# Keeping a feed-forward tile in two PSUM banks, half-width scans and new call orders in a one-core adaLN / attention / feed-forward kernel

## Time and profile before

| | us |
|---|---|
| median of 3 runs (lowest, highest) | 225.58 (223.62, 227.23) |
| the profiled execution: its time, and the span of its instructions | 226.96, 225.0 |
| DVE busy | 190.0 |
| ACT busy | 173.5 |
| PE busy (its matmuls' ends are modelled) | 150.2 |
| POOL busy | 149.4 |

### The profile page before, as it was taken

How to read it: one execution, slowest core, us unless ns; L and a number is a source line. 1 busy time by engine, 2 the same in 40 slices (tenths; PEclk the granted TensorE clock), 3 DMA queues, 4 the chain that set the end, 5 groups by cost and what they waited for, 6 DMA issues and landing times.

```text
span 225.0 us, 2670 instructions
## 1 busy us (share of the span) xinstructions
PE 150.2 (67%) x692; PEld 104.0 (46%) x692; DVE 190.0 (84%) x287; ACT 173.5 (77%) x297; POOL 149.4 (66%) x172
## 2 busy tenths in 40 slices
...
GB/s 199 361 423 143 82 245 0 3 0 0 6 90 0 0 0 0 0 4 0 1 1 0 0 0 3 0 3 1 0 0 1 3 0 0 1 23 25 34 36 70
DMA packets 5439, 9.89 MB, mean 44 GB/s; under 512 B 817, under 2 KB 3505, under 8 KB 5169
## 3 DMA queue, kind: packets, MB, share of 16 engines
...
q10 hardware_dynamic: 368, 0.03, 0.1%
...
## 4 chain that ended last, share of the span: by engine, by line
POOL 15%; PE 13%; issue 10%; DVE 6%; ACT 6%; DVEq 0%; POOLq 0%; ACTq 0%
PE banks L1533 12%; POOL qr L441 2%; POOL wn L498 2%; DVE own L1303 2%; PE banks L1530 2%; POOL grs L441 1%; POOL h L467 1%; ACT junk_q L818 1%; POOL gq L490 1%; DVE Fs L1101 1%; POOL qfl L491 1%; POOL dec L411 1%; ACT w2T L630 1%; POOL qmv L439 1%; POOL stdf L486 1%
## 5 line engine op out<-in xcount | busy, mean ns | idle before, releaser
L411 POOL TENSOR_TENSOR dec<-tri,la 128x1024 f32<-128x1024 f32 x8 | 16.9, 2112 | 15.5 <-DVE la L1179 14.5
L1533 PE MATMUL banks<-inw,uT 128*128 128x8 f32 (+1 forms) x64 | 21.7, 465 | 4.5 <-DVE uT L1147 3.9
L1101 DVE TENSOR_TENSOR_SCAN Fs<-D,E 128x1028 f32<-128x1028 f32 x8 | 18.4, 2320 | 4.6 <-POOL D L375 3.8
L1109 DVE TENSOR_TENSOR_SCAN Ys<-D,Fs 128x1028 f32<-128x1028 f32 x8 | 22.2, 2806 | 0.0
L1533 PE MATMUL banks<-dec,late 128*128 128x512 f32 x32 | 20.0, 754 | 1.8 <-POOL dec L411 1.8
L1533 PE MATMUL banks<-uT,inw 128*128 128x256 f32 x80 | 20.6, 402 | 0.0
L1190 DVE SCALAR_TENSOR_TENSOR cv<-banks,cols,cv 128x255 f32<-128x255 f32 (+2 forms) x48 | 19.2, 473 | 0.1
L1120 DVE SCALAR_TENSOR_TENSOR nd<-Ys,gap,own 128x512 f32<-128x512 f32 x16 | 18.5, 1205 | 0.0
L1533 PE MATMUL banks<-outw,yzT 128*128 128x256 f32 x64 | 16.6, 416 | 2.1 <-ACT yzT L771 2.1
L1533 PE MATMUL banks<-wabs,ones 128*128 128x2 f32 x2 | 0.6, 347 | 25.3 <-ACT dec L618 25.3
L1533 PEld LDWEIGHTS banks<-uT,inw 128*128 128x128 f32 x80 | 15.6, 202 | 3.9 <-issue 2.0
(11 more groups left out here) (176 smaller groups left out, 484.6 us busy)
## 6 DMA issues: line engine op xcount, KB each, us to landing
...
```

What stands on the lines that cost most here:

```text
L411: pool.tensor_tensor(dec[:, c], tri[:].unsqueeze(1).broadcast_to([P, NH, P]), la[:, b % 2, c, :].unsqueeze(2).broadcast_to([P, NH, P]), AL ...
L1101: dve.tensor_tensor_scan(Fs[:, w], D[:, w, 0:L], E[:, b % 2].rearrange("p k c t -> p (k c t)"), 0.0, ALU.mult, ALU.add).then_inc(fs_ok, 1)
L1109: dve.tensor_tensor_scan(Ys[:, w][:, ::-1], D[:, w, 1:L + 1][:, ::-1], Fs[:, w][:, ::-1], 0.0, ALU.mult, ALU.add).then_inc(ys_ok, 1)
L1533: return pe.matmul(dst, lhsT, rhs, start=start, stop=stop)
```

## The change

Four things, all in one edit:

1. Scans in halves. `D` holds one row of decays for both sums (514 + 1), `starts` is half as long, and `forward(b, w, k)`, `backward(b, w, k)` scan 514 elements. `forward(b, w, 0)` waits for `emin_ok` alone, not for POOL's product. `tn` has memory of its own, and `forward` no longer waits for `recip`.
2. The feed-forward tile stays in PSUM. `ffn_mid(i)` is two neighbouring banks. PE writes both halves there and adds `b1` as `diag x b1b` in float32, where `diag` is the identity scaled by `1/al1` (ACT `ffn_diag`; `ral1` comes from one reciprocal more in `ffn_in_back`). ACT's silu takes `al1` as its scale and works in place, gelu too, and `ffn_center` as well; `ffn_center` now waits for `ffn_var` of its own tile. `ffn_shift` reads PSUM and writes `Y`, which takes `U`'s place in `wn`. `ffn_u` is gone.
3. Every bank of `HOME` is new.
4. All five lists are new: the loads' order, two table loads fewer (26), and PE's waits that keep banks apart, among them seven of the form `pe.wait_ge(Y_ok, n)`, which hold PE until `ffn_shift` of tile `n - 1` is done.

```diff
@@ memory and helpers
+        def ffn_mid(i):
+            home = HOME["ffn_up"][i]
+            return banks[:, home:home + 2, :].rearrange("p a n -> p (a n)")
-        starts = sb("starts", [P, CT, T], BF16)
+        starts = sb("starts", [P, T], BF16)
-        D = sb("D", [P, 2, L + 1])
+        D = sb("D", [P, 2, CT * TS + 1])
-        tn = Fs[:, 0, 0:2 * CT * T].rearrange("p (w t) -> p w t", w=2)
+        tn = sb("tn", [P, 2, CT * T])
-        U = wn[:, 0].rearrange("p (i f) -> p i f", i=2)
-        G, Y = GY[:, :, 0], GY[:, :, 1]
+        Y = wn[:, 0].rearrange("p (i f) -> p i f", i=2)
+        diag = sb("diag", [P, 2, P])
+        ral1 = sb("ral1", [P, NT])
-    "ffn_up": ((3, 6), (5, 2), (7, 3), (4, 7), (6, 4), (3, 7), (1, 4), (5, 6)),
+    "ffn_up": (0, 2, 0, 0, 2, 0, 4, 2),
@@ ACT
+            def ffn_diag(i):
+                act.wait_ge(ident_ok, 2)
+                act.wait_ge(al1_ok, 2 * (i // TT + 1))
+                if i >= 2:
+                    act.wait_ge(h_ps, i - 1)
+                act.activation(diag[:, i % 2], ident[:], ACT.Copy, scale=ral1[:, i:i + 1]).then_inc(dg_ok, 1)
             def ffn_silu(i):
-                act.wait_ge(U_ok, 2 * (i + 1))
-                act.activation(U[:, i % 2], U[:, i % 2], ACT.Silu).then_inc(S_ok, 1)
+                act.wait_ge(h_ps, i + 1)
+                act.activation(ffn_mid(i), ffn_mid(i), ACT.Silu, scale=al1[:, i:i + 1]).then_inc(S_ok, 1)
...
@@ DVE
-            def forward(b, w):
-                dve.wait_ge(ev_ok, b + 1)
+            def forward(b, w, k):
+                if k == 0:
+                    dve.wait_ge(emin_ok, b + 1)
+                else:
+                    dve.wait_ge(ev_ok, b + 1)
...
-                if b >= 1:
-                    dve.wait_ge(rn_ok, seeds(b))
-                dve.tensor_tensor_scan(Fs[:, w], D[:, w, 0:L], E[:, b % 2].rearrange("p k c t -> p (k c t)"), 0.0,
-                                       ALU.mult, ALU.add).then_inc(fs_ok, 1)
+                dve.tensor_tensor_scan(Fs[:, w, k], D[:, w, 0:CT * TS],
+                                       E[:, b % 2, k].rearrange("p c t -> p (c t)"), 0.0, ALU.mult,
+                                       ALU.add).then_inc(fs_ok, 1)
...
+                dve.reciprocal(ral1[:, TT * b:TT * b + TT], al1[:, TT * b:TT * b + TT]).then_inc(al1_ok, 1)
-            def ffn_u(i, g):
...
             def ffn_center(i):
                 dve.wait_ge(nmu_ok, i + 1)
+                dve.wait_ge(gvar_ok, i + 1)
                 dve.wait_ge(lng_in, 16)
+                dve.scalar_tensor_tensor(ffn_mid(i), ffn_mid(i), nmu[:, i:i + 1], lngb, ALU.add, ALU.mult)\
+                    .then_inc(W_ok, 1)
...
             def ffn_shift(i):
...
-                dve.scalar_tensor_tensor(Y[:, i % 2], lnbb, std[:, i:i + 1], Y[:, i % 2], ALU.mult, ALU.add)\
+                dve.scalar_tensor_tensor(Y[:, i % 2], lnbb, std[:, i:i + 1], ffn_mid(i), ALU.mult, ALU.add)\
                     .then_inc(Y_ok, 1)
@@ PE
+            def ffn_up(i):
                 pe.wait_ge(wT_ok[0], 1)
                 pe.wait_ge(q1T_ok, i // TT + 1)
+                pe.wait_ge(b1_in, 16)
+                for g in range(2):
+                    half = slice(g * 512, (g + 1) * 512)
+                    for k in range(CT):
+                        mm(ffn_mid(i)[:, half], q1T[:, k, i * P:(i + 1) * P], w1T[:, k, half], k == 0, False)
+                pe.wait_ge(dg_ok, i + 1)
+                for g in range(2):
+                    half = slice(g * 512, (g + 1) * 512)
+                    last = mm(ffn_mid(i)[:, half], diag[:, i % 2], b1b[:, half], False, True)
                 last.then_inc(h_ps, 1)
```

More of the change, by code:

```diff
@@ L581, in _ @@
             ffn_round(5)
+            ffn_dev(7)
             ffn_rms(6)
-            ffn_dev(7)
+            ffn_rms(7)
             ffn_round(6)
-            ffn_rms(7)
             ffn_round(7)
@@ L999, in _ @@
             ffn_var(4)
-            ffn_turned(2, 0)
+            ffn_diag(6)
             ffn_var(5)
```

761 lines of the change are left out of this document (376 added, 385 removed).

## The result

The changed kernel takes **213.09 us** (median of 4, 212.26 to 213.75) against 226.41 (223.62 to 227.8) in the same runs: a ratio of 0.949, 95% interval 0.940 to 0.958. The prediction was 220.7 (212 to 230): the median fell by 13.3 us where 4.9 were forecast, to where the third rival put it. The profiled execution took 213.06; its span is 211.2 against 225.0. The kernel before has two kinds of executions, near 223.7 us at a mean granted clock of 0.92 and near 227 us at 0.89: the profiled one is of the second kind, as most are, so some 3 of the 13.8 us between the two spans go with its lower clock, and the ratio compares the quicker executions alone.

What follows compares the result with a forecast made beforehand. The bound was read as DVE from 14 to 60 us, PE from 123, ACT from 165 to 187, then latency; 1.1 - 3.5 + 1.0 + 0.5 - 4.0 = -4.9 off the median 225.58 gave 220.7 us, range 212 to 230.

Steps and rivals of the forecast that it cites:

- third rival: Whole kernel: DVE is the pacemaker throughout, so its 9.5 us saved count in full; 212.7 us, chance 0.20.
- First part: 14 to 98 us, DVE full: same instructions in another order, half scans +1.9, shorter first_D -0.8; sum +1.1 us.
- The start: First scan up to 2 us sooner, but POOL's own_times_v(0) falls among the scans; together costed at nothing.
- half scans: DVE's scans: splitting adds 0.16 us each, +1.9 for batches 0 to 2 and +0.6 for batch 3.
- 98 to 123 and 123 to 147 us: DVE's wait filled and ffn_u(0) gone, -3.5; then PE full to 165, float32 matmuls against earlier la, net +1.0.
- The hole: Near 102 us: DVE waits 3.57 us for batch 2's features; work moved ahead of that wait was to fill it.
- 147 to 187: ACT full: diags and scale columns +2.7, cheaper make_D; PE's added matmuls covered, if thinly; +0.5 taken.
- The end: From gelu(4) on: two table loads fewer, shift unheld, round(7) starts at 27.6 instead of 31.65; -4.0 us.
- The two loads: At the end, two table loads of 1.28 us fewer on ACT: the largest part of the gain, -2.6.
- DVE between 107 and 205: DVE is the full engine nowhere here, so removing ffn_u's 11.9 us is not a gain by itself.
- First rival: 107 to 165 us: PE becomes the bound as added float32 matmuls fall to half clock, +8.8; 231.8 us, chance 0.16.
- Second rival: From 147 us: a full ACT gets +2.7 and swallows the middle's gains; 224.0 us, no change, chance 0.22.

Runs made afterwards that it cites:

- e13: Kernel before with softplus_out(0), which writes la of batch 0, moved behind the four add_own of batch 1: 225.81 us.
- e15: Changed kernel with softplus_out(0) moved ahead of the four add_own of batch 1, as the kernel before has it: 217.96 us.
- e9: Kernel before with the changed kernel's order of POOL's first calls: 227.47 us.
- e4: Kernel before with each scan as two halves side by side: 225.49 us.
- e3: Changed kernel with whole scans of 1028 again, at the place of the second half: 214.45 us.
- e16: Changed kernel with softplus_out(2) moved five DVE calls back, so la of batch 2 comes 6 us later: 216.03 us.
- e14: Kernel before with softplus_out(0) behind batch 1's add_own and softplus_out(2) ahead of batch 3's backward scans: 228.16 us.
- e12: Changed kernel with diag and the first bias in bf16, so the diagonal matmuls are cheap: 213.28 us.
- e11: Changed kernel with two more table loads on ACT ahead of silu of tile 7: 215.30 us.
- e7: Changed kernel with gelu writing to SBUF, where ffn_var, ffn_center and ffn_shift read it: 222.83 us.
- e5: Kernel before with its sixteen ffn_u left out of DVE's list, first bias and al1 omitted: 227.02 us.
- e8: Changed kernel without the sixteen float32 bias matmuls and the eight ffn_diag, first bias left out: 215.40 us.
- e6: Changed kernel with sixteen unread DVE instructions of about 0.75 us added, waiting for nothing: 220.64 us.
- e10: Kernel before without ffn_u, and with ffn_center and ffn_shift replaced by a maximum over one SBUF operand: 223.64 us.
- e17: Kernel before with softplus_out(0) behind batch 1's add_own, ffn_u out, center and shift replaced by a one-operand maximum: 222.16 us.
- e1: Changed kernel with ffn_u and the feed-forward tile in SBUF back, half scans, banks and other new orders kept: 232.08 us.

## Why the prediction was wrong

- **First part, +1.1 forecast, -4.2 measured: the step that failed**, 5.3 of the 8.9 us that were missed. It said "both DVE lists hold the same instructions in another order" and priced the order at nothing. The instructions are the same, their durations are not: four `add_own` at 4.82 and at 2.71, and the row of `la` between them decides it (e13, e15: 3.5 us at `gated(2)` in the new order). I had read the same hold in the earlier trace rows, with POOL as the one held, and did not ask where POOL holds DVE. The prediction names this as a sign that it is wrong (`gated(2)` moving by over 3 us because DVE and POOL collide otherwise), and that sign came. The start was costed at nothing as well; e9 agrees with that for POOL's order alone. Whether the new lists keep any of the 2.1 us at `gated(0)` is open: with the row put back (e15) `gated(0)` is 2.5 earlier than before and `gated(2)` 0.7. Of the forecast +1.1, the half scans' share is 0.1 in the old order (e4) and 1.0 in the new (e3).
- **98 to 123 and 123 to 147 us**, -3.5 and a part of +1.0, against -3.3 from `gated(2)` to `residual(2)`: the number is right, in part by luck. The hole is gone, but `la(2)` stands 16.2 us earlier where I counted "at least 3", 12.0 of them behind `gated(2)`. e16 gives its worth, 0.5 us per us, in this order; e14 gives none in the other. At 0.5 the 12.0 would be 6.0, an estimate, and 3.3 arrived; what takes the rest is not shown.
- **147 to 187**, +0.5 against -0.2 from `residual(2)` to gelu(4): near nothing in both, by another way. `la(3)` to `residual(3)` grew by 3.6; 1.7 less ahead of it and 2.1 less behind it pay for that. The bias matmuls are 3.8 us of PE there, but with 1.2 (e12) the stretch is only 0.6 shorter, so "covered" is not shown to be wrong, and what the 3.6 are is open.
- **The end, -4.0 forecast, -6.0 measured.** The two loads are as forecast (e11). Mis-sized were the waits for `ffn_up` at half clock: silu(6) was over 8.0 after gelu(4), silu(7) 11.9 and var(7) 18.4, where the sum has 8.9, 13.8 and 20.8. The port was undersized as well: the sum unheld one shift, behind var(7), for 0.3 of its 4.0, and by e7 the hold costs some 4, also ahead of var(7) (silu(7) comes 1.4 later there, behind an `ffn_square` that waits 1.99 for a late shift). The two overlap: e11's 2.7 and e7's 4 are more than the 6.0 together.
- **DVE between 107 and 205**, "the only full engine nowhere": misread, since the earlier trace rows has DVE at 15.54 of 16 from 107 to 123, more than any other engine. The conclusion held even so, in the old order: without `ffn_u` `la(2)` does not come earlier (e5).
- **Half scans**, 0.16 each: nearly nothing on the medians (e3, e4).
- **First rival (PE the bound)**: its mechanism is there, its price is not. PE is in the chain from 146 to 173, and still less of its work makes nothing faster (e8, e12).
- **Second rival (ACT's wall)**: not there. What `la(2)` loses in the middle arrives whole at the end (e16: 3.0 at `residual(2)`, 3.1 on the span), so ACT does not swallow it.
- **Third rival (DVE's work in full)**: the number came within 0.4 us, the reason did not; that is luck. Freed DVE time is worth nothing in the old order (e5) and 7.5 of 12 in the new (e6). What I said for it, that center and shift no longer hold POOL, costs more to take back than DVE's work does (e7: 9.7).
- Signs: DVE 175.2 (near 180 expected; the rest is `add_own`), PE 155.4 (165), 26 loads, `b1b,diag` 0.595 (0.43 to 0.8), POOL's short instructions near 0.2 beside center and shift, 32 us from gelu(4) to the end (34). `project(2)` starts at 135.8, not between 143 and 147. ACT waits for `ffn_up` once in the last 32 us, 0.46 us ahead of silu(6).

What the runs show, then: what the tile in PSUM does for DVE and the port, by the stand-in, is worth 3.5 in the old order (e10), with the one moved row 4.8 (e17); the new orders with the old tile are 5 slower than before (e1); both together gain 13.3. The rest, about 8.5 us, belongs to neither alone. The runs tell what it hangs on (e6, e7, e15, e16: any of four things taken back costs 3 to 10), not how it divides.
